# Layer 1's selective scans: one VectorE instruction for the products with C of both units in PSUM

## The reference

```python
def selective_scan(u, delta, A, Bs, Cs, Dv):
    def step(hc, inp):
        u_t, d_t, B_t, C_t = inp
        hc = hc * jnp.exp(d_t[..., None] * A[None]) + (d_t * u_t)[..., None] * B_t[:, :, None, :]
        return (hc, jnp.einsum('bkdn,bkn->bkd', hc, C_t))
    ...
    _, ys = lax.scan(step, h0, seq)
    return jnp.moveaxis(ys, 0, -1) + u * Dv[None, :, :, None]
```

## Time and profile before

| | |
|---|---|
| median of three runs | 16969.2 us |
| lowest and highest | 16965.33 and 16982.6 us |
| the profiled execution's own time | 16968.33 us |
| its span in the profile | 16966.3 us |
| busy: VectorE, TensorE, GpSimd, ScalarE | 89%, 81%, 74%, 72% |
| mean granted clock of TensorE | 0.921 |
| the two scan stretches of layer 1, from about | 2330 to 6146 us and 6386 to 10205 us |

### The profile page before, as it was taken

How to read it: one execution, slowest core, us unless ns; L and a number is a source line. 1 busy time by engine, 2 the same in 40 slices (tenths; PEclk the granted TensorE clock), 3 DMA queues, 4 the chain that set the end, 5 groups by cost and what they waited for, 6 DMA issues and landing times. The chain is left out here.

```text
span 16966.3 us, 189354 instructions
## 1 busy us (share of the span) xinstructions
PE 13726.7 (81%) x38048; PEld 5660.7 (33%) x38048; DVE 15040.2 (89%) x20527; ACT 12283.9 (72%) x27189; POOL 12583.4 (74%) x6313
## 2 busy tenths in 40 slices
PE   7989978888888878888888886877777767777777
PEld 2222223333333333333333333533333333333333
DVE  6666579999999989999999995889999988999998
ACT  3555567777777757777777774588888858888886
POOL 0000069999999979999999992288988868988886
PEclk9999989999999999999999997988888888888888
DMA  1100023333333333333333332222222212222221
GB/s 24 19 14 16 5 83 111 111 110 111 110 110 110 110 92 110 111 110 111 111 110 110 110 110 64 55 80 83 83 80 81 80 46 80 83 82 82 79 81 47
DMA packets 543207, 1404.94 MB, mean 83 GB/s; under 512 B 135566, under 2 KB 191926, under 8 KB 539430
## 3 DMA queue, kind: packets, MB, share of 16 engines
q1 hardware_dynamic: 542034, 1392.84, 28.2%
HBM read 1311.24 MB, written 58.30 MB: 81 GB/s over the span
## 5 line engine op out<-in xcount | busy, mean ns | idle before, releaser
L1075 PE MATMUL PS<-Hc,ident 128*128 128x448 f32 x16128 | 7407.5, 593 | 1759.3 <-POOL Hc L1416 1422.7
L1407 POOL TENSOR_TENSOR Tr<-du,BC 128x1344 f32<-128x1344 f32 x2688 | 8168.7, 3039 | 33.0 <-DVE du L1277 32.9
L1075 PEld LDWEIGHTS PS<-Hc,ident 128*128 128x128 f32 x16128 | 3092.8, 203 | 5964.8 <-issue 2547.0
L1197 ACT ACTIVATE PS<-dl,A 128x448 f32<-128x448 f32 x5376 | 3401.8, 633 | 1652.4 <-DVE Hr L1325 1057.5
L1416 POOL TENSOR_TENSOR Hc<-Hr,BC 128x448 f32<-128x448 f32 (+1 forms) x2688 | 3567.7, 1327 | 1039.0 <-DVE Hr L1325 968.7
L1325 DVE TENSOR_TENSOR_SCAN PS<-PS,Tr 128x449 f32<-128x449 f32 x3584 | 3712.8, 1078 | 194.4 <-ACT st L1213 184.0
L1332 DVE TENSOR_TENSOR Hc<-PS,BC 128x448 f32<-128x448 f32 x4480 | 2565.7, 606 | 0.0
L1207 ACT ACTIVATE PS<-cs,lneps,A 128x448 f32<-128x448 f32 x2688 | 1942.7, 723 | 112.0 <-DVE PS L1325 92.4
L1325 DVE TENSOR_TENSOR_SCAN Hr<-PS,Tr 128x449 f32<-128x449 f32 x1792 | 1937.0, 1081 | 0.0
L1325 DVE TENSOR_TENSOR_SCAN Hr<-Ar,PS 128x449 f32<-128x449 f32 x1792 | 1930.8, 1077 | 0.0
L1307 DVE SCALAR_TENSOR_TENSOR PS<-PS,Tr 128x448 f32<-128x448 f32 x2688 | 1649.8, 614 | 264.5 <-ACT PS L1207 252.8
(11 more groups left out here) (271 smaller groups left out, 15483.3 us busy)
## 6 DMA issues: line engine op xcount, KB each, us to landing
BC<-bcscratch SPq DMA_DIRECT2D x5376, 224.0 KB, 3.6
zscratch<-zst SPq DMA_DIRECT2D x84, 224.0 KB, 1.9
bcscratch<-rows SPq DMA_DIRECT2D x336, 56.0 KB, 2.9
z<-zscratch SPq DMA_DIRECT2D x28, 672.0 KB, 4.8
xg<-mid SPq DMA_DIRECT2D x12, 1176.0 KB, 8.1
xr<-mid SPq DMA_DIRECT2D x56, 168.0 KB, 2.7
rl<-rows SPq DMA_DIRECT2D x56, 168.0 KB, 3.3
Q<-part SPq DMA_DIRECT2D x72, 98.0 KB, 4.4
```

Of the source, the lines that this page charges most:

```text
L1075: e.matmul(PS[:, YB + c, 0:T], K["ident"][:], Hc[:, g % NHC, c, :], start=False, stop=(nn == 15)).then_inc(y_done, 1)
L1197: e.activation(decay_at(u, 1), dl[:, q % 2, c, :], ACT.Exp, scale=A[:, q // NT, c, nn:nn + 1]).then_inc(a_done, 1)
L1407: e.tensor_tensor(Tr[:, g % NTR] if ratio else Tr[:, g % NTR, :, 1:TW], du[:, q % 2], b, ALU.mult).then_inc(t_done, 1)
```

## The change

`project` of VectorE no longer takes a unit. It waits until the second of the two scans into PSUM is done, and for TensorE to have read both units of the Hc buffer; then one instruction multiplies both banks with C, which is read twice (a broadcast over the units), and raises h_done by the number of units. In layer 3 that number is 1, and the instruction is as wide as before. Nothing else is changed; the waiters for h_done count as before.

```diff
-            def project(g, c):
-                e.wait_ge(s_done, 3 * g + c + 1)
+            def project(g):
+                e.wait_ge(s_done, 3 * g + ON_DVE)
                 if g >= NHC:
-                    e.wait_ge(y_done, 3 * (g - NHC) + c + 1)
-                e.tensor_tensor(Hc[:, g % NHC, c, :], state_at(g, c, 1), BC[:, g % NBS, 1, :], ALU.mult).then_inc(h_done, 1)
+                    e.wait_ge(y_done, 3 * (g - NHC) + ON_DVE)
+                c_ = BC[:, g % NBS, 1:2, :].broadcast_to([128, ON_DVE, T])
+                e.tensor_tensor(Hc[:, g % NHC, 0:ON_DVE, :], PS[:, HB:HB + ON_DVE, 1:TW], c_,
+                                ALU.mult).then_inc(h_done, ON_DVE)
...
                 scan(g, 1)
                 if q + 1 < NQS:
                     prepare(q + 1, 3 * r + 1)
-                for c in range(ON_DVE):
-                    project(g, c)
+                project(g)
                 if ratio and g + 1 < NG:
                     input2(3 * g + 3)
                 scan(g, 2)
```

## The result

The changed kernel takes 17192.8 us (median of four runs, 17179.6 to 17202.9) against 16967.7 us before: a ratio of 1.0132, with a 95% interval of 1.0117 to 1.0147. It is slower, as forecast, but by 225 us where 105 were predicted, and it lies above the stated range. The profiled execution of after has a span of 17185.2 us, 218.9 us more than the 16966.3 us of before.

What follows compares the result with a forecast made beforehand. VectorE was taken to bound the kernel in layer 1's scans. Waiting loses 0.124 us a step, merging saves 0.057; the 0.067 left, over 14 x 112 steps, adds 105 us to 16968: 17073 us, range 17030 to 17130.

Steps and rivals of the forecast that it cites:

- What bounds the kernel, and the sign: Layer 1's scan stretches: VectorE, busy 89% of the span, sets the pace; the change makes the kernel slower, chance 0.85.
- What is lost by waiting: Product directly behind scan(g, 1): starts 0.034 us after its end instead of 0.09 before, 0.124 us lost a step.
- rival 3: Merged product costs more through two banks, a third pattern dimension or raising by two: saving gone, 17162 us; chance 0.06.
- What is saved by merging: Layer 1's products: one merged product takes 1.073 us against 1.13 for the pair, 0.057 us saved a step.
- The step: One step of layer 1's scans on VectorE becomes 0.067 us longer, from 4.02 to 4.087 us.
- How much reaches the end: In each block of layer 1's scans, 14 of 16 steps pass the loss on: 14 x 112 x 0.067 = 105 us.
- the pauses ahead of L1325: VectorE's idle time ahead of the scans into PSUM was to shrink by some 15 us.
- pause of L1277: VectorE's 0.33 us idle in layer 1's preparation; forecast kept it, while the 17050 us end was said to absorb both.
- What moves and costs nothing: Unit 0's products come 0.55 us later, but TensorE, ScalarE and GpSimd wait no longer for it; layer 3 changes by zero.
- rival 4: The change misbehaves, above all unit 0's late products holding up TensorE: 56 us on top of 105, 17129 us; chance 0.03.
- Rival 1: The product's wait behind its scan costs nothing, only the 0.057 us saving stays: 16872 us, faster by 0.6%; chance 0.09.
- Rival 2: Pauses from ScalarE's or TensorE's chain absorb the loss, less than a third passes: 16990 us, within 0.2%; chance 0.06.

Runs made afterwards that it cites:

- the first experiment: The changed kernel, but each merged product raises h_done by one instead of two and its waiters count steps; 17083.8 us, ratio 1.0066.

## Why the prediction was right and wrong

**What bounds the kernel, and the sign: right.** VectorE holds the step; an instruction moved directly behind the one that feeds it costs more than the merging saves.

**What is lost by waiting: this step failed, by the size of its term.** I put the whole loss at 0.124 us a step; it is 0.18 us. I read 0.034 us from the earlier trace rows and took it for any wait. The chain there has one wait for each tap, which the tap carries itself. The merged product cannot, since it raises by two. I had named that as part of rival 3, but priced it as a lost saving and gave it 0.06 together with two other causes. Measured: 0.093 us where I had 0.034, 0.059 us a step more; that is the greater part of the miss of 120 us, and it is what the first experiment gave back (109 us, with 0.059 x 1792 x 0.89 = 94 us as the estimate). The row that would have told me was in the trace of before: the 0.103 us ahead of L497.

**What is saved by merging: 13 ns too much here.** I had 0.057 us a step, and by the starts it is 0.044 (below). For the product's duration 1.073 us was predicted and 1.092 us measured. The slope was right within 8 ns, for the product lasts 1.065 us where nothing delays it. The rest belongs to the pause ahead, and I had the row that hints at it: in the earlier trace rows a scan behind a pause lasts 1.10 us, in the earlier trace rows a scan lasts 1.078 on average.

The Trainium skill, "VectorE: DVE Perf Modes", section "The TRN2 errata — SBUF-src ops pay a fixed extra latency per instruction", gives (N + 151) / 0.96 ns for a tensor_tensor in fp32. As an estimate from that page, 896 elements take 1091 ns, which agrees with the 1092 behind a pause and not with the 1065 without one. The products here read one operand from PSUM, which the formula does not name.

**The step.** 4.02 to 4.087 predicted; measured 4.15. By the starts: the products begin 0.18 us later against the end of the scans (0.09 ahead, 0.09 behind), and from their start to that of scan(g, 2) it is 1.01 us (3508.58 to 3509.59) instead of 1.05 (3511.10 to 3512.15): 0.04 saved.

**How much reaches the end: nearly right.** I let 14 of 16 steps pass the loss on, 0.875. With 0.137 us a step (0.18 less 0.044, from the starts) and 1792 steps, 245 us, the spans' 218.9 us are 0.89. I expected the pauses ahead of L1325 to give 15 us; they gave 35. The lower end of the forecast, 17050 us, takes one absorbed pause of L1277 a block, as the 55 waits of the earlier trace rows have it, and not both; with both it would be 17043 us, and neither changes the outcome.

**What moves and costs nothing: right.** VectorE has no new waits for Hc or st, and TensorE's idle time ahead of L1075 rose only from 1759 to 1819 us in a span 219 us longer. TensorE does wait longer for VectorE's products (its matmuls 686 us against 335), but less for GpSimd's (1128 us against 1423). Unit 0's products end 0.67 us later against the end of the scans; my own terms would have given 0.59, not the 0.55 that I wrote. Layer 3's products are as they were (896 of 0.598 us without idle time). So rival 4 is out.

**The rivals.** Rival 1 (the wait costs nothing) fell with every kernel whose product stands directly behind its scan. The rule of the Trainium skill that I quoted for it, "VectorE: DVE Perf Modes", section "The DRAIN you can't avoid", does not hold here: the swapped narrow products differ from the kernel before in their order and their readers' waits alone, and cost 229 us, most of it by a gap of 0.034 us in place of an overlap of 0.09. Rival 2 (the pauses take it up) fell, since 0.89 of the loss arrives. Rival 3 was the nearest in its time (17162 us) and had the true cause among its three, but its mechanism, a product of over 1.13 us, did not come; the second bank and the repeated row were tested and cost nothing.

## What to carry to other kernels

Before you merge two short instructions on a saturated engine, ask what the first of them covered: if it stood between a producer and its consumer, the merged one has the whole wait exposed, here 0.12 to 0.2 us against 0.04 to 0.07 us saved. Where such a wait can't be avoided, let the instruction carry it itself: name the wait that comes last first, and raise the semaphore by one, so that the others go into semaphore instructions that are fulfilled early. And look in the trace at what an instruction waits for itself before you take its gap as the price for another.

## What the runs showed of the hardware that I had not expected

Between two VectorE instructions of which the second needs the first, the gap depends on where the wait stands: 0.034 us in the instruction, 0.093 to 0.106 us in one semaphore instruction ahead, 0.23 us in the first of two (its two semaphore instructions stand 0.1 us apart). With no such need the second begins 0.08 to 0.09 us before the end of the first. An instruction that raises a semaphore by two carries no wait in these programs: none of the 1792 merged products of after does, and none of the 4480 narrow ones in each of the two kernels that raise by two. Behind a pause a product lasts longer: 1.092 against 1.065 us for 896 elements, and 0.023 us more for a pair of 448.
